# Sorted experts: when results are fetched back, and how far apart the shared groups stand

## The reference

```python
logits = x @ gate_w.T                       # 8 experts
scores = softmax(logits);  topk_w, topk_i = top_k(scores, 2)
topk_w = topk_w / topk_w.sum(-1) * 2.5
y      = sum over the two chosen experts e of
         topk_w * ((silu(x @ w_gate[e]) * (x @ w_up[e])) @ w_down[e])    # width 176
shared = (silu(x @ sw_gate) * (x @ sw_up)) @ sw_down                     # width 352
out    = layernorm(x + y + shared)
```

## Time and profile before

| what | us |
|---|---|
| median of 3 runs (range) | 2119.89 (2117.36 to 2120.77) |
| profiled execution, its own time | 2114.67 |
| its span | 2112.9 |
| busy PE / DVE / ACT / POOL | 1958.9 / 1527.1 / 1259.4 / 1336.8 |
| mean granted TensorE clock | 0.97 of full |
| expert stage, first block's turn | from 1690.86 |

### The profile page before, as it was taken

How to read it: one execution, slowest core, us unless ns; L and a number is a source line. 1 busy time by engine, 2 the same in 40 slices (tenths; PEclk the granted TensorE clock), 3 DMA queues, 4 the chain that set the end, 5 groups by cost and what they waited for, 6 DMA issues and landing times. The chain is left out here.

```text
span 2112.9 us, 47421 instructions
## 1 busy us (share of the span) xinstructions
PE 1958.9 (93%) x15991; PEld 1703.1 (81%) x15991; DVE 1527.1 (72%) x4046; ACT 1259.4 (60%) x3812; POOL 1336.8 (63%) x1459
## 2 busy tenths in 40 slices
PE   6888859999999999999999999999999999999655
PEld 4555449999999999999999999998999878888544
DVE  5999956777777777777777777778777655555445
ACT  3565536666666666666666666666666544444334
POOL 5899937666666666666666666666666654444445
PEclk9999979999999999999999999999999989999867
DMA  4200000000000000000000000001000122222335
GB/s 135 63 18 18 16 25 6 9 21 17 16 14 21 15 16 15 20 15 18 15 16 20 17 16 14 21 17 35 15 19 16 39 58 81 78 73 71 87 87 158
DMA packets 105022, 75.78 MB, mean 36 GB/s; under 512 B 11044, under 2 KB 98676, under 8 KB 104660
## 3 DMA queue, kind: packets, MB, share of 16 engines
q1 hardware_dynamic: 93732, 53.66, 9.1%
q0 software_dynamic: 8640, 17.97, 2.5%
q10 hardware_dynamic: 2416, 1.12, 0.2%
HBM read 40.15 MB, written 32.57 MB: 34 GB/s over the span
## 5 line engine op out<-in xcount | busy, mean ns | idle before, releaser
L1026 POOL TENSOR_TENSOR x_prob<-x_prob,x_inv 128x496 f32<-128x496 f32 x514 | 521.7, 1015 | 459.6 <-DVE x_inv L1176 457.0
L1104 ACT ACTIVATE x_prob<-x_ps_S,x_nmax 128x248 f32<-128x248 f32 x1028 | 472.8, 467 | 225.6 <-DVE x_nmax L1170 223.7
L1170 DVE TENSOR_REDUCE x_nmax<-x_ps_S 128x2 f32<-128x496 f32 x515 | 344.9, 670 | 105.1 <-PE x_ps_S L848 97.0
L1118 ACT COPY x_probT<-x_ps_T 124x512 f32<-124x512 f32 x512 | 300.3, 587 | 166.7 <-PE x_ps_T L1358 164.0
L846 PE MATMUL x_ps_S<-x_kT_lo,x_G_hi 128*128 128x248 f32 x1030 | 328.6, 319 | 0.0
L1358 PE MATMUL x_ps_T<-ident,x_prob 128*124 128x128 f32 x2048 | 319.0, 278 | 7.9 <-POOL x_prob L1026 6.4
L1358 PEld LDWEIGHTS x_ps_T<-ident,x_prob 128*124 128x124 f32 x2048 | 233.1, 140 | 74.1 <-POOL x_prob L1026 30.3
L848 PE MATMUL x_ps_S<-x_kT_hi,x_G_hi 128*128 128x248 f32 x1030 | 285.9, 278 | 0.0
L847 PE MATMUL x_ps_S<-x_kT_hi,x_G_lo 128*128 128x248 f32 x1030 | 285.5, 277 | 0.0
L1328 PE MATMUL x_ps_O<-x_probT,x_V 124*64 124x128 f32 x4096 | 251.9, 276 | 0.4 <-ACT x_probT L1118 0.4
L1595 POOL DMA_INDIRECT sorted_results<-e_y,w_wkv x142 | 149.2, 1051 | 158.9 <-DVE e_y L1719 149.2
(11 more groups left out here) (240 smaller groups left out, 4491.1 us busy)
## 6 DMA issues: line engine op xcount, KB each, us to landing
w_wkv<-sorted_rows SPq DMA_DIRECT2D x142, 66.0 KB
e_back<-sorted_results SPq DMA_DIRECT2D x28, 256.0 KB, 3.5
x_nk<-latents SPq DMA_DIRECT2D x34, 124.0 KB
latents<-lin_nlat SPq DMA_DIRECT2D x32, 128.0 KB, 1.8
turned_rows<-w_rows SPq DMA_DIRECT2D x32, 128.0 KB, 1.7
w_wq<-turned_rows SPq DMA_DIRECT2D x32, 128.0 KB
out_dram<-e_result SPq DMA_DIRECT2D x16, 256.0 KB, 2.4
x_nk<-in_ctx SPq DMA_DIRECT2D x34, 120.0 KB, 2.3
```

The lines of the kernel that those rows point to most:

```text
L1026: nc.gpsimd.tensor_tensor(prob[:, k], prob[:, k], inv[:, k].unsqueeze(2).broadcast_to([P, 2, K]), ALU.mult).then_inc(prob_ready, 1)
L1104: nc.scalar.activation(prob[:, k, h, :], ps_S[:, n % BANKS, h * K:(h + 1) * K], ACT.Exp, bias=nmax[:, k, h:h + 1], accum_out=total[:, k, h ...
L1118: nc.scalar.copy(probT[0:KT, s % (2 * GANG)], ps_T[0:KT, s % 2, :]).then_inc(probT_ready, 1)
L1170: nc.vector.tensor_reduce(nmax[:, k, :], ps_S[:, n % BANKS, 0:2 * K].rearrange("p (h k) -> p h k", h=2), AX, ALU.max, negate=True).then_in ...
```

## The change

The transfers of the first twelve groups are issued twelve steps before the addition of their halves instead of five, and BACK_TIME for them is now 115, 117, 120, 122, ... 142 (2.5 steps apart) instead of 112, 115, ... 145. The last four are at 152, 154, 156, 158 instead of 155, 157, 159, 161, and the program has three steps less (167). The first fourteen shared groups start nine steps apart (8, 17, ... 125) instead of eight, so that each has one more step without a piece and the fourteenth ends at step 132, not 119. Their preparation and loads move with them. ScalarE issues the transfers of groups 14 and 15 at step 148 instead of 153.

```diff
     SHARED_FROM = 8
+    EVERY = 9
...
-    BACK_TIME = [FIRST_BLOCK[1] + 9 + 3 * g if g < WHOLE else TOTAL + 13 + 2 * (g - WHOLE) for g in range(GROUPS)]
+    AHEAD = 12
+    BACK_TIME = [FIRST_BLOCK[1] + AHEAD + 5 * g // 2 if g < WHOLE else TOTAL + 10 + 2 * (g - WHOLE) for g in range(GROUPS)]
...
-                g, k = divmod(t - SHARED_FROM, PIECES)
-                if g >= GROUPS - LATE:
+                g, k = divmod(t - SHARED_FROM, EVERY)
+                if g >= GROUPS - LATE or k >= PIECES:
                     return None, None
...
-            starts = [SHARED_FROM + PIECES * g for g in range(GROUPS)]
+            starts = [SHARED_FROM + EVERY * g for g in range(GROUPS)]
...
-                g = back_at(t, -5, -5)
+                g = back_at(t, -AHEAD, -AHEAD)
                 if g is not None and g < WHOLE:
...
-                if t == TOTAL + 11:
+                if t == TOTAL + 6:
                     sent_after(act, TOTAL)
                     for g in (WHOLE + 2, WHOLE + 3):
```

## The result

The changed kernel takes 2088.92 us (median of 4 runs, 2085.96 to 2091.13) against 2119.72 for the kernel before; the ratio is 0.9855 (95% interval 0.9838 to 0.9872). It is 30.8 us faster. Forecast were 51.7 us less, 2068.2, with a range of 2055 to 2084: the direction was right and the time outside the range. The profiled execution ran 2088.56 with a span of 2086.7, where the sum gave 2061.2: 25.5 us are to be found. By the medians 20.7 are missing. The profiled execution before lay 5.2 us under its median and the one after only 0.4, so up to 4.8 of the 25.5 can be spread between executions.

A forecast was written before the change was run, and what follows sets the result against it. Late returned results were taken to bound the stretch, a loop of 11.5 us per three blocks. Span 2112.9-47.9-3.8=2061.2, plus 1.8 beyond the span, 2063.0; plus 5.2 to the median, 2068.2 us, range 2055 to 2084.

The forecast's parts named there:

- part 1: Results' transfers twelve steps ahead: GpSimd's wait for the transfer goes in all twelve groups, seven steps giving 16 us.
- I take nothing for the queue: SyncE's queue behind the results' transfers: load_rows and stores standing there were given no cost.
- part 2: Shared groups nine apart: eleven steps without a piece before step 115, 1.7 us each, costing 18.7 us.
- part 3: Steps 115 to 144: waits gone, 2.5 us a step, 75 us in all; gain 47.9 us by step 145.
- upper bound of 2.73: Steps 115 to 144: us a step if none of the saved scatter is seen, 13.67/5.
- rival A: Steps with results: GpSimd and VectorE in lockstep, 2.75 to 3.1 us a step, 2076 to 2086 us; chance 0.2.
- two nearly full engines that wait for each other seldom reach either one's limit: Steps 115 to 144: reason given for taking 2.5 us a step, between bounds of 2.28 and 2.73.
- buy work for the last stretch: Before step 115: eleven steps without a piece cost 18.7 us and leave shared work for the later steps.
- part 4: The end: two additions, not three, behind the last shared sum; gain 3.8 us, bounds +3.8 and -1.
- C: Results' transfers still late, 1.6 to 2.7 us in each of twelve groups: 2087 to 2100 us; chance 0.06.
- D: Expert stage: thinner steps drop TensorE to the low clock, slower, 2163 us if a third is low; chance 0.03.
- B: Everything overlaps: 2.2 to 2.28 us a step, thin steps 1.45, 2056 to 2059 us; chance 0.12.

The follow-up runs named there:

- store_first: Changed kernel with SyncE's stores put ahead of load_rows in a step; 2083.1 us, ratio 0.9833 to the kernel before.
- close32: Changed kernel with the closing transfers on SyncE at step 32 instead of 30; 2082.07 us, ratio 0.9829 to the kernel before.
- combo: Changed kernel with closing transfers at step 32 and stores ahead of load_rows; 2078.45 us, ratio 0.9817 to the kernel before.
- ahead_store: Changed kernel with shared groups eight steps apart and stores ahead of load_rows; 2076.88 us, ratio 0.9812 to the kernel before.
- the last pair: Changed kernel, stores first, ScalarE's last transfers at step 153, VectorE's addition two steps behind GpSimd's; groups eight apart 2072.8 us, nine apart (closing at 32) 2074.44.

## Why the prediction missed

**Transfers ahead (part 1): right on the transfer, wrong on the queue.** All twelve waits for a transfer went. The first sentence that failed is "I take nothing for the queue". It counted what the transfers wait for and what SyncE does behind them, but of the stores only whether their result is ready, not who waits for the store to be done. Group 4's normalisation does, and the store moved from step 120 to 123, while the normalisation moved by only one step (130 to 131). Price: 4.7 us by the ratios of store_first (3.7 between the profiles' steps 115 and 145).

**Nine steps apart (part 2): the thin step was sized nearly right, a collision was missed.** A period took 1888.77-1867.83=20.9 us, forecast 20.8; eleven of them make 1.6 us more. The failing step is that loads "move with them" at no price. Load 4 fell behind the closing transfers: 5.5 us by the ratios of close32, 6.6 in the profiles. The rest before step 115 is 2.1 us that are there when step 8 begins (before anything changed; the kernels run here began it between 1710.5 and 1713.5), and about 1 us in close32's 250.6 that I can't place.

**Steps 115 to 144 (part 3): the step that failed most.** The term is 30x2.5=75 us, where 87.5 were measured. With no store wait over 2 us (combo) it was still 84.5 us, 2.82 a step, over the prediction's own upper bound of 2.73. Thirty steps in 74.8 us exist (ahead_store), but in the schedule with eight steps between groups, almost without pieces: that the number is the forecast's is luck. Of the 12.5 us too much, 3.7 are the store wait. Some 7 went with a second step of distance between the two additions (83.8 to 76.7 us): VectorE's wait for GpSimd's (3.6 us), and what comes with it (the clock, 0.91 to 0.96, and VectorE's new order), which no run takes apart. That is rival A, in its mechanism as far as shown and in its size (2.75 to 3.1 a step, chance 0.2). Of its signs the additions 7 us apart came (7.2), a GpSimd without gaps did not: that engine stood 22.4 us for VectorE's copies of results. So what failed is the sentence that chose the middle because "two nearly full engines that wait for each other seldom reach either one's limit". Neither engine was nearly full (75% and 68%); the cost lay in the waits between them, and the sum had only the engines' rates. About 2 us of the 12.5 are not placed. The shut-out of VectorE at step 124 is 1 us at most, and the clock (0.88 here, 0.99 before it) falls in the same stands, so I can't price it apart. The words "buy work for the last stretch" (part 2) failed too: the shared pieces did not run in idle time, and in every pair of kernels their work came on top (9.7 us in combo against ahead_store, 7.5 in the last pair).

**The end (part 4): the crowd.** The prediction had the fourth group's data at 11.5 us after the issue and in time. It was, but the first two came late. The issue, the addition of group 13 and the last shared sum, in the changed kernel:

```profile
2062.46 2.02 SPq L1503 DMA_DIRECT2D e_back<-sorted_results  x4
...
2071.62 1.27 POOL L1604 TENSOR_TENSOR e_back<-e_back 128x512 f32<-128x512 f32 x1 [2.59 <-DMA e_back<-sorted_results]
...
2075.74 0.68 DVE L1744 TENSOR_TENSOR X<-X,e_ps_s 128x512 f32<-128x512 f32 x1
```

GpSimd's addition of group 13 began 9.2 us after the issue, not 6.4, and group 13's addition and moments held the last shared sum on VectorE; its last product had ended at 2073.3. Two additions stood behind that sum, as forecast. Putting ScalarE's issue back gave 1.5 us of the 1.6 missing in the nine-step version.

**The rivals.** C fell: no wait for a transfer before step 145. D fell: the clock was 0.99 with a thin step in nine, and the missing hundredth is the stand at step 43. B fell: the thirty steps took 2.92 us each in the changed kernel. The range was too narrow at its upper end because its bounds were all rates of engines. The two single waits, about 10 us together, had no place in it.

## What to carry to other kernels

When steps are moved in a program written out by hand, list for every queue each neighbour it lands behind, and for every transfer who waits for its end, buffers that it frees included; here a move of four steps for a load and three for a store cost about 5 us each. Idle time shown beside a stall is not room for more work: take the stall away first and look again, since the work shifted there (some pieces of two shared groups) was worth nothing once the transfers were early. Where a consumer one step behind its producer waits for it, try a second step of distance, if the buffers allow; here neither engine was full, and it gave 5 to 7 us.

## What the hardware showed

Eight transfers of 66 KB each into DRAM held SyncE's queue for 9.1 us (1.14 each), where three loads of 66 KB take 2.6 and two transfers of 256 KB 1.0. After a stand of 3.28 us TensorE's products of one step took 0.63 us instead of 0.39, the lower of the two clock levels. An operation of VectorE on four elements a partition (L1766) took 2.06 us beside GpSimd's scatter and addition, 0.17 at its shortest:

```profile
2052.29 2.06 DVE L1766 TENSOR_SCALAR e_vare<-e_mom 128x4 f32<-128x4 f32 x1
...
2053.02 1.28 POOL L1604 TENSOR_TENSOR e_back<-e_back 128x512 f32<-128x512 f32 x1
```
